# A three-phase decoder layer on one core: the last phase's token tiles turned by VectorE blocks and transfers inside SBUF

## The reference

```python
logits = jnp.einsum('bsh,he->bse', x, router_w) + router_b + load_balancer
rw, sel = jax.lax.top_k(logits, K)                       # 2 of 4 experts
e0 = jax.nn.silu(x @ sw_w1) * (x @ sw_w3) @ sw_w2
eq = x @ me_eq_w + me_eq_b
sym = (eq @ me_wv + me_bv) @ me_wo + me_bo
e1 = jax.nn.gelu(sym @ me_c1w + me_c1b, approximate=False) @ me_c2w + me_c2b
syn = x @ ce_syn_w + ce_syn_b
attn = (syn @ ce_wv + ce_bv) @ ce_wo + ce_bo
h2 = _layer_norm(syn + attn, ce_n1g, ce_n1b)
ff = jax.nn.relu(h2 @ ce_f1w + ce_f1b) @ ce_f2w + ce_f2b
h2 = _layer_norm(h2 + ff, ce_n2g, ce_n2b)
e2 = h2 @ ce_gen_w + ce_gen_b
e3 = jax.nn.gelu(x @ ml_w1 + ml_b1, approximate=False) @ ml_w2 + ml_b2
```

## Time and profile before

| | us |
|---|---|
| median of 3 runs | 1550.42 (1549.96 to 1550.51) |
| span of the profiled execution | 1550.1 |
| PE busy | 1502.6 (97%) |
| DVE busy | 1139.4 (74%) |
| ACT busy | 847.5 (55%) |
| POOL busy | 372.8 (24%) |

### The profile page before, as it was taken

How to read it: one execution, slowest core, us unless ns; L and a number is a source line. 1 busy time by engine, 2 the same in 40 slices (tenths; PEclk the granted TensorE clock), 3 DMA queues, 4 the chain that set the end, 5 groups by cost and what they waited for, 6 DMA issues and landing times.

```text
span 1550.1 us, 28824 instructions
## 1 busy us (share of the span) xinstructions
PE 1502.6 (97%) x11288; PEld 1065.1 (69%) x11288; DVE 1139.4 (74%) x2305; ACT 847.5 (55%) x1123; POOL 372.8 (24%) x404
## 2 busy tenths in 40 slices
PE   8999999899999999999999999999999999999998
PEld 4333333335566666666656898888989898888887
DVE  6445555548799999999967877777676767777675
ACT  5888889876688888888863421222222221222221
POOL 1000000124556667666453300000000000000000
PEclk9999999999899999999999999999999999999999
DMA  7656665446565666657652100000000000000000
GB/s 153 137 112 117 122 121 103 71 95 113 95 93 88 105 89 98 110 78 96 93 169 69 62 1 15 1 14 1 1 15 1 14 1 15 1 15 1 1 14 14
DMA packets 61576, 97.37 MB, mean 63 GB/s; under 512 B 12461, under 2 KB 29881, under 8 KB 61441
## 3 DMA queue, kind: packets, MB, share of 16 engines
q1 hardware_dynamic: 61312, 95.34, 33.3%
q10 hardware_dynamic: 128, 0.20, 0.0%
HBM read 26.29 MB, written 4.19 MB: 20 GB/s over the span
## 4 chain that ended last, share of the span: by engine, by line
PE 84%; DVE 8%; ACT 3%; SPq 3%; issue 2%; DMA 1%; POOLq 0%; DVEq 0%; POOL 0%; ACTq 0%
PE ps L109 79%; SPq L119 3%; PE ps L1277 2%; DVE NM L1495 2%; ACT H L614 1%; ACT PX L1438 1%; DVE EE L758 1%; PE ps L1239 1%; DVE XC L2106 1%; PE ps L1285 1%; PE ps L1914 0%; DMA ST<-QS 0%; PE ps L1905 0%; PE ps L1209 0%; DVE QS L678 0%
## 5 line engine op out<-in xcount | busy, mean ns | idle before, releaser
L1495 DVE TENSOR_REDUCE NM<-ps 128x4 f32<-128x1024 f32 x256 | 307.5, 1219 | 29.2 <-PE ps L109 27.7
L1438 ACT ACTIVATE PX<-ps 128x1024 f32<-128x1024 f32 x256 | 262.2, 1024 | 80.2 <-PE ps L109 79.0
L614 ACT ACTIVATE H<-ps,b1c 128x1024 f32<-128x1024 f32 x256 | 268.2, 1118 | 48.6 <-PE ps L109 47.0
L2066 ACT ACTIVATE GF<-ps,cols 128x512 f32<-128x512 f32 x128 | 88.2, 689 | 295.7 <-PE ps L109 295.6
L109 PE MATMUL ps<-XC,W_sw_w 128*128 128x512 f32 x768 | 185.8, 393 | 0.0
L2257 DVE CAST GH<-GF 128x512 fp32r<-128x512 f32 x192 | 82.0, 427 | 106.9 <-ACT GF L2066 101.8
L109 PEld LDWEIGHTS ps<-XC,W_sw_w 128*128 128x128 f32 x768 | 140.5, 188 | 28.0
L2365 POOL TENSOR_SCALAR RSc<-AGc 128x4 f32<-128x4 f32 x23 | 6.9, 298 | 599.5 <-DVE AGc L2152 599.5
L109 PE MATMUL ps<-PX,VT 128*32 128x256 f32 x2048 | 138.6, 388 | 0.1
L2259 DVE TENSOR_TENSOR GH<-GF,GH 128x512 fp32r<-128x512 f32 x192 | 133.2, 694 | 6.6
L109 PE MATMUL ps<-KT,QT 48*128 48x512 f32 x512 | 128.1, 498 | 3.7 <-DVE NM L1495 1.8
(11 more groups left out here) (240 smaller groups left out, 2560.3 us busy)
## 6 DMA issues: line engine op xcount, KB each, us to landing
KT<-KS SPq DMA_DIRECT2D x128, 192.0 KB, 4.7
ST<-QS SPq DMA_DIRECT2D x254, 96.0 KB, 2.8
QT<-XSb SPq DMA_DIRECT2D x128, 96.0 KB, 4.2
XT<-in_xT_dram SPq DMA_DIRECT2D x8, 512.0 KB, 4.1
raw_a<-in_x_dram SPq DMA_DIRECT2D x8, 512.0 KB, 4.3
CR<-in_ctxT_dram SPq DMA_DIRECT2D x8, 512.0 KB, 4.7
out_dram<-X SPq DMA_DIRECT2D x7, 512.0 KB, 2.9
R_sw_w<-in_sw_w_dram SPq DMA_DIRECT2D x6, 512.0 KB, 5.5
```

The costliest lines, as they stand in the source:

```text
L614: e.activation(H1[s % 8][:, :, :], PP[s % 3][:, :, :], ACT.Tanh, bias=b1c[:, half:half + 1], scale=1.0).then_inc(act_th, 1)
L1438: e.activation(PX[s % 3][:, :, :, :], PP[2][:, :, :].rearrange("p g (c q) -> p g c q", c=2), ACT.Exp, bias=0.0, scale=0.25).then_inc(act_e ...
L1495: e.tensor_reduce(NM[u % 2][:, qc, :, :, i], PP[qc][:, :, :].rearrange("p g (m k) -> p g m k", m=2), AX.X, ALU.max, negate=True).then_inc( ...
L2066: e.activation(g[:, :], o, f, bias=cols[:, col:col + 1], scale=1.0).then_inc(act_g, 1)
```

## The change

In phase_c PE turns only the first X1 and the first NN. The other 22 tiles are turned in two steps. DVE transposes every 32x32 block of the tile where it stands into TT (turn, one instruction of 128x4x8x32), which leaves the blocks in the wrong partitions. SP then moves the blocks: 16 transfers for a tile, each of 32 partitions x 2 x 512 B (32 KB), from TT to XR. ACT and DVE make hi and lo from XR in SBUF with a pattern that undoes the order of the blocks (turned, as_turned). TT and XR are one buffer each, for all three kinds of turn.

- N is turned at chunk 1, behind center, and split at 5 as before.
- R is turned at chunk 16, behind center, and split at 20 as before.
- The next pair's X is turned at chunk 8 (TURN_X) and split at 11 (SPLIT_X) into a second XH, since the first is still in use. At chunk 23 nothing is loaded any more, and second() of chunk 21 stands at its regular place, behind first() of the next pair's chunk 0.

The program is also built with dynamic_dma_scratch_size=1024, which makes room in SBUF. The core of the diff:

```diff
-def in_bank(j):
-    return (3, 2) if j == 0 else (7, 6)
+IN_BANKS = (3, 2)
+TURN_X, SPLIT_X = 8, 11
...
-    XH = Place(M, 65536)("XC", [128, 2, 2, TOK], F32R)
+    put = Place(M, 176192)
+    XH = [Place(M, 65536)("XC0", [128, 2, 2, TOK], F32R), put("XC1", [128, 2, 2, TOK], F32R)]
+    TT = put("TT", [128, 8, 4, 32])
+    XR = put("XR", [128, 2, TOK])
...
+    def as_turned(ap):
+        return ap.rearrange("p (v a t) -> p a v t", v=4, a=4)
+    def turned(c):
+        return XR[:, c, :].rearrange("p (a v t) -> p a v t", a=4, v=4)
+    def n_turn(j):
+        return max(3 * j, 0)
+    def x_turn(j):
+        return 3 * j - 2
+    def r_turn(j):
+        return 3 * j + 2 if j + 1 < NP else 3 * j + 1
...
+        def turn():
+            for a in range(4):
+                for b in range(4):
+                    dma(e, XR[32 * b:32 * b + 32, :, 128 * a:128 * a + 128],
+                        TT[32 * a:32 * a + 32, b::4, :, :].rearrange("p c v t -> p c (v t)"), d_turn)
         def rest():
-            for j in range(NP - 1):
-                w.wait_ge(dve_ctr, out_stats(j) + 1)
-                dma(e, out_tm[:, 4 * j:4 * j + 4, :], X1[:, 4 * j:4 * j + 4, :], d_out)
+            for j in range(NP):
+                if j:
+                    w.wait_ge(dve_turn, n_turn(j))
+                    w.wait_ge(dve_gt, 2 * j)
+                    turn()
+                    w.wait_ge(dve_ctr, out_stats(j - 1) + 1)
+                    dma(e, out_tm[:, 4 * j - 4:4 * j, :], X1[:, 4 * j - 4:4 * j, :], d_out)
+                if j + 1 < NP:
+                    w.wait_ge(dve_turn, x_turn(j + 1))
+                    w.wait_ge(dve_nt, 2 * j + 2)
+                    turn()
+                w.wait_ge(dve_turn, r_turn(j))
+                w.wait_ge(dve_nt, 2 * j + 2)
+                w.wait_ge(dve_x, 2 * min(j + 2, NP))
+                turn()
...
-        def turn_n(j):
-            w.wait_ge(dve_ctr, syn_stats(j) + 1)
+        def turn_n():
+            w.wait_ge(dve_ctr, syn_stats(0) + 1)
             for c in range(2):
                 w.wait_ge(*free[7 - c])
                 for i in range(4):
                     t = e.transpose(P[7 - c][:, 128 * i:128 * i + 128], NN[:, i, 128 * c:128 * c + 128], ident)
                 t.then_inc(pe_nt, 1)
-                free[7 - c] = (dve_nt, 2 * j + c + 1)
-
-        def gen_turn(j):
-            w.wait_ge(dve_ctr, ff_stats(j) + 1)
-            for c in range(2):
-                w.wait_ge(*free[7 - c])
-                for i in range(4):
-                    t = e.transpose(P[7 - c][:, 128 * i:128 * i + 128], RR[:, i, 128 * c:128 * c + 128], ident)
-                t.then_inc(pe_gt, 1)
-                free[7 - c] = (dve_gt, 2 * j + c + 1)
+                free[7 - c] = (dve_nt, c + 1)
         def generate(j):
             w.wait_ge(dve_gt, 2 * j + 2)
...
         def work(j, i):
             first(j, i)
-            if i == 5:
-                turn_n(j)
-            if i == 20:
-                gen_turn(j)
+            if i == 5 and not j:
+                turn_n()
             if i == 22:
                 generate(j)
             if i >= LAG:
                 if i < 23 or j + 1 < NP:
                     second(24 * j + i - LAG)
-            elif i and j:
+            elif j:
                 second(24 * j + i - LAG)
-            if i == 23 and j + 1 < NP:
-                load_x(j + 1)
-                second(24 * j + 21)
...
+        def next_x(j):
+            w.wait_ge(b_end["normalised"], NP)
+            w.wait_ge(pe_a, 24 * (j - 1))
+            w.wait_ge(d_turn, 256 * x_turn(j))
+            for c in range(2):
+                e.activation(as_turned(XH[j % 2][:, c, 0, :]), turned(c), ACT.Copy).then_inc(act_x, 1)
...
                 w.wait_ge(pe_gen, 4 * j)
+                if j:
+                    w.wait_ge(d_turn, 256 * n_turn(j))
                 for c in range(2):
-                    w.wait_ge(pe_nt, 2 * j + c + 1)
-                    e.activation(NTh[:, c, :], P[7 - c], ACT.Copy).then_inc(act_nt, 1)
+                    if j:
+                        e.activation(as_turned(NTh[:, c, :]), turned(c), ACT.Copy).then_inc(act_nt, 1)
+                    else:
+                        w.wait_ge(pe_nt, c + 1)
+                        e.activation(NTh[:, c, :], P[7 - c], ACT.Copy).then_inc(act_nt, 1)
             if i == 20:
                 w.wait_ge(pe_a, 24 * j + 12)
+                w.wait_ge(d_turn, 256 * r_turn(j))
                 for c in range(2):
-                    w.wait_ge(pe_gt, 2 * j + c + 1)
-                    e.activation(NTh[:, c, :], P[7 - c], ACT.Copy).then_inc(act_gt, 1)
-            if i == 23 and j + 1 < NP:
-                load_x(j + 1)
+                    e.activation(as_turned(NTh[:, c, :]), turned(c), ACT.Copy).then_inc(act_gt, 1)
+            if i == SPLIT_X and j + 1 < NP:
+                next_x(j + 1)
...
+        def next_x(j):
+            hi, lo = XH[j % 2][:, :, 0, :], XH[j % 2][:, :, 1, :]
+            for c in range(2):
                 w.wait_ge(act_x, 2 * j + c + 1)
-                e.tensor_tensor(XH[:, c, 1, :], P[b], f32(XH[:, c, 0, :]), ALU.subtract).then_inc(dve_x, 1)
+                e.tensor_tensor(as_turned(lo[:, c, :]), turned(c), f32(as_turned(hi[:, c, :])), ALU.subtract).then_inc(dve_x, 1)
...
+        def turn(n, tile):
+            w.wait_ge(d_turn, 256 * (n - 1))
+            e.transpose(TT[:, :, :, :].rearrange("p b v t -> p v b t"), tile.rearrange("p v (b t) -> p v b t", b=8)).then_inc(dve_turn, 1)
+        def turn_n(j):
+            w.wait_ge(dve_ctr, syn_stats(j) + 1)
+            turn(n_turn(j), NN[:, :, :])
+        def turn_x(j):
+            w.wait_ge(b_end["normalised"], j + 1)
+            turn(x_turn(j), X1[:, 4 * j:4 * j + 4, :])
+        def turn_r(j):
+            w.wait_ge(dve_ctr, ff_stats(j) + 1)
+            turn(r_turn(j), RR[:, :, :])
...
+        def low_r(j):
+            for c in range(2):
+                w.wait_ge(act_gt, 2 * j + c + 1)
+                e.tensor_tensor(as_turned(NTl[:, c, :]), turned(c), f32(as_turned(NTh[:, c, :])), ALU.subtract).then_inc(dve_gt, 1)
...
-                turned(act_nt, j, dve_nt)
+                low_n(j)
             if i == 20:
-                turned(act_gt, j, dve_gt)
+                low_r(j)
             if i == 22:
                 generate(j)
-            if i == 23 and j + 1 < NP:
-                load_x(j + 1)
+            if i == TURN_X and j + 1 < NP:
+                turn_x(j + 1)
+            if i == SPLIT_X and j + 1 < NP:
+                next_x(j + 1)
             if i == 3 and j:
                 w.wait_ge(dve_add, ADDS * j)
                 stats(out_stats(j - 1), X1[:, 4 * j - 4:4 * j, :])
...
             if i == 16:
                 center(ff_stats(j), RR)
+                turn_r(j)
```

More of the change, by code:

```diff
@@ L1763, in phase_c @@
     d_out = M.sem("c_out")
+    d_turn = M.sem("c_turn")
     pe_x = M.sem("c_pe_x")
@@ L1794, in phase_c @@
     dve_ff = M.sem("c_dve_ff")
+    dve_turn = M.sem("c_dve_turn")
     dve_seq = M.dve_seq
@@ L1873, in tensor, with load_x @@
         free[0] = free[1] = (b_end["folds"], 12)
[L1875 to L1879, removed]
+        def load_x():
+            w.wait_ge(b_end["normalised"], 1)
+            for c, b in enumerate(IN_BANKS):
                 for i in range(4):
-                    t = e.transpose(P[b][:, 128 * i:128 * i + 128], X1[:, 4 * j + i, 128 * c:128 * c + 128], ident)
+                    t = e.transpose(P[b][:, 128 * i:128 * i + 128], X1[:, i, 128 * c:128 * c + 128], ident)
                 t.then_inc(pe_x, 1)
-                free[b] = (dve_x, 2 * j + c + 1)
+                free[b] = (dve_x, c + 1)
         def synergy(j):
@@ L1944, in first @@
             b = first_bank(i)
-            hi, lo = XH[:, :, 0, :], XH[:, :, 1, :]
+            hi, lo = XH[j % 2][:, :, 0, :], XH[j % 2][:, :, 1, :]
             if x == "sw":
@@ L2032, in scalar, with load_x @@
         w = Passed(e)
-        def load_x(j):
+        def load_x():
             w.wait_ge(b_end["scores"], 240)
[L2036 to L2039, removed]
+            for c, b in enumerate(IN_BANKS):
+                w.wait_ge(pe_x, c + 1)
+                e.activation(XH[0][:, c, 0, :], P[b], ACT.Copy).then_inc(act_x, 1)
+        def next_x(j):
[4 more added lines that the diff above has]
+                e.activation(as_turned(XH[j % 2][:, c, 0, :]), turned(c), ACT.Copy).then_inc(act_x, 1)
         def take(name, q):
@@ L2087, in early @@
             if s == INPUT + 1:
-                load_x(0)
+                load_x()
             if s in EARLY:
@@ L2101, in vector, with load_x @@
         seq = Chain(w, dve_seq)
-        def load_x(j):
-            for c, b in enumerate(in_bank(j)):
-                w.wait_ge(act_x, 2 * j + c + 1)
-                e.tensor_tensor(XH[:, c, 1, :], P[b], f32(XH[:, c, 0, :]), ALU.subtract).then_inc(dve_x, 1)
+        def load_x():
+            for c, b in enumerate(IN_BANKS):
+                w.wait_ge(act_x, c + 1)
```

(29 more changed lines are left out.)

6 lines of the change are left out of this document (2 added, 4 removed).

## The result

The changed kernel takes 1596.03 us (median of 4 runs, 1592.27 to 1600.43), the kernel before 1550.47 (4 runs, 1549.96 to 1552.56). The ratio is 1.0299, with a 95% interval of 1.0282 to 1.0316: slower. The forecast was 1589.

A forecast was written before the change was run, and what follows sets the result against it. TensorE was taken to bound the last phase, with VectorE tight at chunks 11 to 14. The sum -19.5 + 6 x 6.2 + 8 x 2.6 + 0.4 = +38.9 us gave 1589 us, range 1544 to 1612.

The forecast's parts named there:

- What goes: TensorE loses 22 groups of transposes at 0.79 us and a 0.30 us wait before synergy in 7 pairs: 19.5 us gained.
- C: Time from SP's start on a tile's 16 transfers to the landed tile: 12.3 us, bounds 8.4 and 13.3.
- the rivals: Other outcomes: cheap issue (0.20), issue hidden behind the landing (0.04), VectorE's transposition at 2.44 us or slowed landings (0.18).
- cheap issue: Rival: SP issues the new transfers at a spacing below 0.44 us, making the kernel faster, 1541 to 1556; chance 0.20.
- the rule of the Trainium skill that I weighed: Initiating a DMA is usually short beside the DMA itself; by it C would be near 2.7 us.
- A: TensorE's wait for ff_add before chunk 12's second layer, from X's late tile: C - 6.1, 6.2 us in 6 pairs.
- G: TensorE's wait before generate, from R's turn between chunks 16 and 20: C - 9.7, 2.6 us in 8 pairs.
- the likeliest case: The forecast itself, 1589 us, given chance 0.58 and the range 1575 to 1602.

The follow-up runs named there:

- n_only: Kernel before with only N of pairs 1 to 7 turned by VectorE and 16 transfers, X and R staying on TensorE; 1544.86 us, ratio 0.9956.
- r_on_pe_split21: Changed kernel with R given back to TensorE and the next X, transposed at chunk 8, split at chunk 21 instead of 11; 1539.02 us, ratio 0.9930.
- half_the_transfers: Changed kernel with 8 transfers of 64 KB a turn instead of 16 of 32 KB, half of the blocks landing in wrong places; 1540.69 us, ratio 0.9937.
- fill_the_wait: Changed kernel with 16 extra matmuls, results unread, on TensorE in the gap ahead of chunk 12's second layer; 1590.06 us, ratio 1.0249.
- split15: Changed kernel with the next X split at chunk 15 instead of 11, still transposed at chunk 8; 1566.44 us, ratio 1.0090.
- turn5_split10: Changed kernel with the next X transposed at chunk 5 instead of 8 and split at chunk 10 instead of 11; 1568.97 us, ratio 1.0101.

## Why the prediction was right, and where its sizes were off

**What goes: right.** Synergy starts 1114.40 - 1112.97 = 1.43 us after the second layer ahead of it, where the earlier trace rows have 1.82; I had put 0.30 on that, and it is 0.39. n_only gains 0.87 us a group and r_on_pe_split21 2.01 a pair, where the terms say 0.79 and 1.88.

**C: right in kind, 0.8 too long.** The issue is as forecast from the earlier trace rows: 597 ns in the median for 590, some 9.6 us from the first to the last. The landing took 1.9 us; I had taken 2.7 from the earlier trace rows. VectorE's transposition, which no row showed, takes 1.24 us; I had taken 1.22. That disposes of the rivals: cheap issue needed 0.44 us, and the rule of the Trainium skill that I weighed (DMA: Bandwidth & Descriptors, "Issuing engines are not separate DMA queues") does not hold for such a row of small transfers: one alone takes 0.60 us to issue and 1.9 to land, but of the row's 11.46 us 9.6 is issue. half_the_transfers shows the same from the other side.

**A: right for six pairs, wrong for the first.** Six waits of 5.1 to 6.2 us, 5.6 in the mean, were forecast as 6.2. But the first pair pays 4.4 us too, and I had given it 0.4, on the word that its chunks 8 to 10 are spread over the end of the phase before. That gave the chunks room, but not the split of the next X: it waits for POOL's last normalisation of the phase before. ACT's copy there:

```profile
886.32 1.15 ACT L2070 ACTIVATE XC<-XR 128x512 fp32r<-128x512 f32 x2 [5.94 <-POOL X L1664]
```

Its first transfer started at 874.29, so the tile itself was not there much before either. half_the_transfers tells the two apart: its chain is some 5 us shorter, ACT there too waits for POOL (5.90 us), and TensorE loses 4.39 us where it lost 4.44. So in this pair POOL is enough to cause the wait.

**G: too large, from C and from the time that R's chain has.** 2.6 was forecast; 9.7 / 8 = 1.2 us was measured. With C = 11.46 the formula gives 1.8. R's own 16 transfers took longer in the pair shown, 12.1 us from VectorE's end to ACT's start (1093.07 to 1105.15), which would make 2.4. But the formula took the time from the end of R's centring to generate from the kernel before, 1090.8 - 1077.9 = 12.9 us, and that is 13.8 after (1091.78 to 1104.20 + 1.39), which brings it to 1.5; the row has 1.42. The slow groups behind A are not the reason: fill_the_wait, where the clock stays up in six of seven gaps, has the same 13.8 us in its pair and 10.3 / 8 = 1.3 us of G. split15 and turn5_split10, where A is gone, have 2.1 and 2.2. So A itself goes with a smaller G. In the two pairs looked at, VectorE's centring no longer waits for POOL (0.93 us in the earlier trace rows); that this is all of it is argued, not shown.

**The clock: missing.** The step "TensorE is 6.2 us late: A" priced an idle TensorE by its idle time alone. The rows after show 1.4 to 2.6 us more in each of 7 pairs, 14.2 us, and fill_the_wait takes most of it away. The Trainium skill (TensorE: Matmul & The Clock Gate, "Part 1: The HAM clock gate") states that an idle TensorE falls to 1.2 GHz and comes back to 2.4 under sustained work. The trace agrees: 0.50 and then 1.00. Had I weighed that page when A came out at 6 us, I would have looked for a price of the fall; with the 2.0 us a gap measured since, the forecast would have been 12 us higher.

**The sum again, with what was measured:** -19.5 for what goes, +37.8 for A in 7 pairs, +9.7 for G, +14.2 for the clock, +1.2 in the first pair, is +43.4. The span grew by 41.4, but in these two executions SP came to the weights of "ml" 3.6 us earlier after than before (865.63 for 869.20), so the last phase grew by 45.0, and 1.6 us of it are not assigned. The forecast of +38.9, where the medians differ by 45.6, was that near because errors cancel, and that is luck: what it lacked, the clock and the first pair (14.2 + 4.0 + 1.2 = 19.4), against what it had too large, A in six pairs (37.2 for 33.4) and G (20.8 for 9.7), together 14.9. The 1596.03 lies in the likeliest case's own range.

## What to carry to other kernels

A tile moved in pieces costs the issuing queue one issue a piece, here 0.6 us whatever the size, so count issues before bytes and merge pieces first. A chain that is as long as this one belongs only where its consumer has that much room, and what stands behind the consumer on its engine must have it too: the same 16 transfers made TensorE wait over 5 us a pair for ff_add with the split at chunk 11, and not at all with it at chunk 15 or 21. And where a forecast makes TensorE idle at a stretch, price the clock behind the gap too: here 1.4 to 2.6 us behind each stop of 4.4 to 6.2, and about 1.5 behind some of the stops of 1.7 to 2.7.

## What the hardware showed that I had not expected

- In these runs the size of an SBUF-to-SBUF transfer hardly entered its price: 32 KB on 32 partitions 597 ns to issue and 1.9 us to land, 64 KB on 64 partitions 607 ns and 2.0 us.
- VectorE transposes the 32x32 blocks of a 128x1024 fp32 tile in 1.24 to 1.25 us, about the 1.22 us of the multiply of the same size in the earlier trace rows.
- TensorE stopped at about 1078.7, and the granted clock was down to 0.50 before it started again at 1083.87. After work came back it read 0.50, 0.61 and then 1.00 from 1088. In fill_the_wait it had stopped for only 2.15 us there and read 1.00 from 1082 to 1088.
- A short stop can be enough. In split15 TensorE waited 1.77 us, started again at 918.83, and the granted clock averaged 0.59 in the stretch from 920 to 922; behind a wait of 2.51 us in the same run (to 1099.45) it stayed at 1.00. The kernel before, n_only and r_on_pe_split21, where TensorE waits 1.2 us once or not at all from 880 us on, read 1.00 from there until the last matmuls are done.
